# Starting the second half of an expert layer with the two experts whose split weights are still in the ring

## The reference, cut to what matters

```python
x = layernorm(x + linear_attention(x))          # "first" steps b, n
x = layernorm(x + x0_experts(x, token_ids))     # 4 experts, picked by token id
x = layernorm(x + golden_ffn(x))                # f0: 8 experts, all run on all tokens
x = layernorm(x + group_attention(x))           # steps a*.2 to a*.12
x = layernorm(x + cross_attention(x, ctx))      # steps a*.13 to a*.18
x = layernorm(x + moe(x))                       # f1: routed experts and a shared one
```

```python
gate = einsum('btd,edf->betf', x, Wg);  up = einsum('btd,edf->betf', x, Wu)
e_out = einsum('betf,efd->betd', silu(gate) * up, Wd)
out = einsum('bte,betd->btd', weights, e_out)   # weights: the golden router
```

## Time and profile before

| what | value |
|---|---|
| median of three runs | 465.72 us (464.29 to 471.58) |
| the profiled execution: its time | 466.7 us |
| its span, from first to last instruction | 464.9 us |
| outside the span | 1.8 us |
| PE busy | 439.1 us, 94% of the span |
| DVE, ACT, POOL busy | 248.5, 247.2, 261.5 us (53 to 56%) |
| mean granted clock of TensorE | 0.985 |
| transfers | 35.22 MB, 76 GB/s on average |

### The profile page before, as it was taken

The page is one execution under the profiler, slowest core; times in us unless marked ns, Lnnn a source line. Parts: engine busy times, 40 slices in busy tenths (PEclk is TensorE's granted clock), DMA queues, the critical chain, the costliest instruction groups (busy, mean ns, idle before and its releaser), DMA issues.

```text
span 464.9 us, 9286 instructions
## 1 busy us (share of the span) xinstructions
PE 439.1 (94%) x3668; PEld 367.4 (79%) x3668; DVE 248.5 (53%) x625; ACT 247.2 (53%) x424; POOL 261.5 (56%) x217
## 2 busy tenths in 40 slices
...
DMA packets 15672, 35.22 MB, mean 76 GB/s; under 512 B 2028, under 2 KB 5996, under 8 KB 15629
## 3 DMA queue, kind: packets, MB, share of 16 engines
...
q10 hardware_dynamic: 476, 0.63, 0.5%
...
HBM read 33.05 MB, written 1.05 MB: 73 GB/s over the span
## 4 chain that ended last, share of the span: by engine, by line
PE 56%; DVE 4%; ACT 3%; POOL 2%; issue 2%; ACTq 0%; POOLq 0%; DVEq 0%
PE bank L435 11%; PE bank L438 9%; PE bank L436 9%; PE bank L679 5%; PE bank L681 5%; PE bank L680 5%; PE bank L753 2%; PE bank L636 2%; PE bank L741 1%; DVE stats L1301 1%; ACT x_tok L905 1%; POOL rstd L1156 1%; PE bank L725 1%; PE bank L727 1%; PE bank L726 1%
## 5 line engine op out<-in xcount | busy, mean ns | idle before, releaser
L1190 POOL TENSOR_TENSOR h_lo<-hraw,h_hi 128x512 fp32r<-128x512 f32 x76 | 97.8, 1290 | 66.4 <-ACT h_hi L992 66.1
L435 PE MATMUL bank<-xT_hi,pk_hi 128*128 128x512 f32 x256 | 106.1, 414 | 4.0 <-DVE hraw L1476 3.2
L436 PE MATMUL bank<-xT_hi,pk_lo 128*128 128x512 f32 x256 | 101.9, 398 | 1.3 <-issue 1.3
L992 ACT ACTIVATE h_hi<-hraw 128x512 fp32r<-128x512 f32 x76 | 47.8, 629 | 86.3 <-DVE hraw L1476 79.0
L1476 DVE TENSOR_TENSOR hraw<-bank,sil 128x512 f32<-128x512 f32 x76 | 52.3, 689 | 64.0 <-PE bank L438 30.6
L1196 POOL TENSOR_TENSOR pk_lo<-pk_raw,pk_hi 128x512 fp32r<-128x512 f32 (+1 forms) x44 | 74.5, 1694 | 19.1 <-ACT pk_hi L1010 19.0
L438 PE MATMUL bank<-xT_lo,pk_hi 128*128 128x512 f32 x256 | 81.5, 400 | 0.0
L679 PE MATMUL bank<-pk_hi,h_hi 128*128 128x256 f32 x272 | 78.0, 287 | 2.0 <-DVE x_tok L1490 2.0
L681 PE MATMUL bank<-pk_hi,h_lo 128*128 128x256 f32 x272 | 76.8, 283 | 0.0
L680 PE MATMUL bank<-pk_lo,h_hi 128*128 128x256 f32 x272 | 76.8, 282 | 0.0
L435 PEld LDWEIGHTS bank<-xT_hi,pk_hi 128*128 128x128 f32 x256 | 48.7, 190 | 21.9 <-issue 8.8
...
## 6 DMA issues: line engine op xcount, KB each, us to landing
...
```

Source lines behind the costliest of these rows:

```text
L435: pe.matmul(o, w(kc)[0], x(kc)[0], start=kc == 0, stop=False)
L436: pe.matmul(o, w(kc)[1], x(kc)[0], start=False, stop=False)
L992: A(h_hi[:, row, at * 512:(at + 1) * 512], hraw[:, s % 2, :], ACT.Copy).then_inc(sems["hid_hi"], 1)
L1190: pool.tensor_tensor(h_lo[:, row, q], hraw[:, s % 2, :], h_hi[:, row, q].bitcast(F32), ALU.subtract).then_inc(sems["hid_lo"], 1)
```

## The change

The second half of f0 begins with experts 6 and 7, whose split weights are still in the two slots, and goes on with experts 0 to 5. The function `expert` gives the expert of a unit, and DVE takes the router's weights by it. Packs of f0 are numbered 0 to 13 apart from the units (`pack_f0`), and a slot may be overwritten after the last unit that uses its pack (`last_use`). The packs of f1 then have numbers from 14. `chunk`, `pack_f1` and `last_use` are written for f1 as well, but with `RF1 = 0` and both tuples in plain order nothing changes there. Two transfers of 512 KB and two of 256 KB fall away, and with them two copies of each kind on ACT and two subtractions of each kind on POOL. The matmuls are the same in number and size. The five tables of orders are written anew throughout.

```diff
+PK0, RF1 = 2 * E0 - 2, 0
...
+def expert(m):
+
+    return (m if m < E0 else m - 2) % E0
+
+FIRST, SECOND = tuple(range(N1)), tuple(range(N1))
...
+def again(j, n, r):
+
+    return j if j < n else j - r
+
+def last_use(i, n, r):
+
+    return i if i < n - r else i + r
+
+def pack_f0(m):
+    return again(m, E0, 2)
...
-    return ("f0", i) if i < 2 * E0 else ("f1", i - 2 * E0)
+    return ("f0", i) if i < PK0 else ("f1", i - PK0)
...
 DVE_ORDER = """
-p0 b0.0 b0.1 b0.2 b0.3 b0.4 b0.5 p2 b0.6 b0.7 p5 b0.8 b1.0 b1.1 n0.0 b1.2 b1.3 b1.4 b1.5 b1.6 b1.7 n0.2 b1.8 m0 m1
+p0 b0.0 b0.1 b0.2 b0.3 b0.4 b0.5 p2 b0.6 b0.7 b1.0 b0.8 p5 n0.0 b1.1 b1.2 b1.3 b1.4 b1.5 b1.6 b1.7 n0.2 m0 b1.8 m1 m2
...
                 elif u < U_F1:
-                    pe.wait_ge(sems["g_lo"], u - U_F0 + 1)
+                    pe.wait_ge(sems["g_lo"], pack_f0(u - U_F0) + 1)
...
-                    pe.wait_ge(sems["d_lo"], m + 1)
-                    chunks, wh, wl = KC, d_part("f0", m, pk_hi), d_part("f0", m, pk_lo)
+                    i = pack_f0(m)
+                    pe.wait_ge(sems["d_lo"], i + 1)
+                    chunks, wh, wl = KC, d_part("f0", i, pk_hi), d_part("f0", i, pk_lo)
...
                 elif kind == "f0" and i >= 2:
-                    act.wait_ge(sems["up_ready"], up_no(S_F0 + 2 * (i - 2) + 1))
+                    act.wait_ge(sems["up_ready"], up_no(S_F0 + 2 * last_use(i - 2, E0, 2) + 1))
...
-                    act.wait_ge(sems["out_ready"], out_no(U_F0 + i - 2))
+                    act.wait_ge(sems["out_ready"], out_no(U_F0 + last_use(i - 2, E0, 2)))
...
-                    weights, e, h = gold, (u - U_F0) % E0, (u - U_F0) // E0
+                    weights, e, h = gold, expert(u - U_F0), (u - U_F0) // E0
```

More of the change, by code:

```diff
@@ L107 @@
+G17 G18 S4 G19 G20 G21 G22 G23 G24 G25 R1 G26 G27 G28 G29 G30 G31 G32 G33 G34 G35 G36 G37 G38 G39 G40 G41 O0
 """.split()
 PE_ORDER = """
-b0.0 b0.1 b0.2 b0.3 b0.4 b0.5 b0.6 b0.7 b1.0 b0.8 b1.1 b0.9 b1.2 b1.3 b1.4 b1.5 b1.6 b1.7 n0.2 b1.8 g0 g1 b1.9 g2 g3
-d0 g4 n1.2 g5 g6 d1 g7 g8 d2 g9 g10 d3 g11 g12 d4 g13 r0.2 d5 g14 r0.3 g15 g16 u16 d6 g17 d7 u17 g18 u18 g19 u19 d8
-g20 u20 g21 u21 r1.2 d9 r1.3 g22 u22 g23 d10 u23 g24 u24 g25 u25 g26 u26 g27 d11 u27 d12 g28 u28 g29 d13 u29 g30 u30
-g31 u31 d14 d15 g32 u32 g33 u33 a0.2 g34 u34 a0.3 a0.4 d16 a0.5 a0.6 a0.7 g35 a0.8 u35 g36 u36 g37 u37 d17 a0.10 g38
@@ L118 @@
-u74 g75 u75 d48 d49 d50 d51
+b0.0 b0.1 b0.2 b0.3 b0.4 b0.5 b0.6 b0.7 b1.0 b0.8 b1.1 b0.9 b1.2 b1.3 b1.4 b1.5 b1.6 b1.7 n0.2 b1.8 g0 g1 g2 b1.9 g3
+g4 d0 g5 g6 n1.2 d1 g7 g8 d2 g9 g10 d3 g11 g12 d4 g13 g14 r0.2 d5 g15 g16 r0.3 d6 u16 g17 u17 g18 d7 u18 g19 d8 u19
+g20 u20 g21 u21 d9 g22 u22 g23 d10 u23 g24 u24 g25 d11 u25 g26 r1.2 u26 g27 r1.3 d12 u27 g28 u28 g29 u29 d13 g30 u30
+g31 u31 g32 d14 u32 d15 g33 u33 g34 u34 a0.2 g35 u35 a0.3 a0.4 d16 g36 a0.5 a0.6 a0.7 d17 a0.8 u36 g37 u37 g38 u38 g39
@@ new lines @@
+u39 a0.10 d18 a0.25 g40 u40 a0.11 g41 a0.26 d19 u41 g42 u42 g43 u43 a0.14 d20 a0.15 g44 u44 a0.16 g45 u45 a0.17 g46
+a0.18 d21 u46 g47 u47 a0.21 d22 a0.22 d23 g48 u48 g49 u49 g50 u50 a1.2 d24 d25 a0.24 a1.3 a1.4 g51 u51 a1.5 a1.6 a1.7
+d26 a1.8 g52 u52 g53 u53 g54 u54 a1.10 d27 a1.25 d28 g55 a1.11 u55 a1.26 g56 u56 d29 d30 g57 u57 g58 a1.14 d31 d32
+a1.15 u58 d33 a1.16 g59 u59 a1.17 d34 a1.18 g60 u60 g61 u61 a1.21 d35 d36 a1.22 g62 u62 d37 g63 u63 g64 a1.24 u64 g65
+d38 d39 u65 g66 u66 g67 d40 u67 d41 d42 g68 u68 g69 d43 u69 g70 u70 g71 d44 d45 u71 g72 d46 u72 g73 u73 g74 u74 g75
@@ L141 @@
+D40 G41 l71 l72 l73 l74 D41 l75 y0 y1
 """.split()
 DVE_ORDER = """
[L143 to L146 removed]
```

106 lines of the change are left out of this document (54 added, 52 removed).

## The result

The changed kernel takes 470.1 us (median of 4 runs, 468.6 to 470.9); the kernel before, run beside it, 466.1. The ratio is 1.0094, 95% interval 1.0053 to 1.0135. A second series gave 470.45 against 465.79, ratio 1.0084 (1.0046 to 1.0122). The forecast was 464.7, in a range that ended at 468.5. The profiled execution took 470.9 us, its span is 469.1, against 466.7 and 464.9 before.

The account below looks back on a forecast made before the run. PE was taken as the bound, busy 439.1 of 464.9 us. Terms 1.8 + 0.3 - 0.3 - 3.9 + 1.1 = -1.0 took the profiled 466.7 to 465.7, median forecast 464.7 us, range 460.5 to 468.5.

Parts of the forecast that it names:

- New pause before `g2`: Start of f0: `g2` must wait for `m0`, as `b1.9` no longer hides that chain; +1.8 us, bounds 0 and 2.5.
- End of f0's first half: Old pauses of 3.1 us go, new ones before `g31` and `d15` total 3.4; +0.3 us, bounds -3.1 and +1.5.
- `d15`'s: End of f0's first half: a new pause of 2.2 us before `d15`, with `c` taken at 5.55 us.
- Just enough: Before `g21`: PE's 8.5 us of work would cover the 8.3 us of `m18`, router block 0 and `m19`.
- Attention of the first half: Wait at `a0.14` 2.3 us where 3.0 were lost, plus 0.4 for another pause; -0.3 us, bounds -3.0 and +1.7.
- Both sides of that sum: First half's attention: 2.3 us lost by waiting instead of 3.0, against 0.4 for a pause like `g40`'s elsewhere.
- Start of f1: Around `u49`, `g50`: shorter pauses, no low clock, +0.65 for a new `a1.2` wait; -3.9 us, bounds -4.7 and -1.5.
- Smaller ones: Cross attention +0.3, `a1.14` +0.3, pauses between the second half's small matmuls +0.5; +1.1 us together.
- the other two parts: Cross attention's read has less work ahead of it, +0.3 us; `a1.14` has less work over its chain, +0.3 us.
- the second: Rival, chance 0.2: new pauses before `g2` and `d15` also bring low clock, 1.7 us each; 468.1 us.
- The fourth: Rival, chance 0.1: waits behind `u50`, `a1.2` or `a1.3` grow as `u49`'s shrinks; -1.5 for -3.9, 467.1 us.
- term 4: Start of f1: the gain of -3.9 us from shorter pauses before `u49` and `g50` and no low clock.

Follow-up runs that it names:

- e15: Changed kernel with the old start up to `g10`, `h10`, `l8`, `a2`, but ScalarE's `S0` left in its changed place behind `h2`: median 471.6 us.
- e12: Changed kernel repeated with no edit, for a second trace and more runs: semaphore pauses the same to 0.01 us; its median is not given.
- e4: Changed kernel with one GpSimd step moved, `S3` behind `a1.0` instead of ahead of it: gain 0.9 us at equal clock.
- e5: Changed kernel with three GpSimd steps moved away from VectorE's router blocks, `D2` behind `l19`, `D7` behind `l29`, `S3` behind `l48`: median 470.0 us.
- e7: Old order tables without the two dropped packs, with one VectorE swap, `m48` ahead of `a1.0`: median 468.2 us.
- e9: Old tables without two packs; `m48`, `G16` ahead of `a1.0`, `m49` behind; `g50`, `u50` ahead of `a1.2`; `h48`, `h49` ahead of `a1.1`; `S3` behind `l48`: median 465.5 us.

## Why the prediction was wrong, point by point

1. *New pause before `g2`, +1.8*: 1.65. Right; e15 got 1.1 of it back.
2. *End of f0's first half, +0.3*: the old pauses went (3.16) and `g21` 1.14 and `g31` 1.46 came, `d15`'s not: -0.56. The net was near, two parts were wrong for one reason. Block 0 was taken at 6.8 us from the earlier trace rows; here it takes 7.8 (112.09 to 119.91), with 2.1 us of waiting for GpSimd. "Just enough" was not. And `c`, "5.55 us, measured", held 2.6 us of such waits: it takes 2.9 us (169.28 to 172.22) in the changed kernel, so `d15` waits for nothing. The rows of `c`'s longest instruction, before (with GpSimd's beside it) and after:

```profile
157.58 2.77 DVE L1365 TENSOR_SCALAR cap<-cap 128x1024 f32<-128x1024 f32 x1
...
157.40 2.39 POOL L1196 TENSOR_TENSOR pk_lo<-pk_raw,pk_hi 128x1024 fp32r<-128x1024 f32 x1
```

```profile
171.25 0.70 DVE L1402 TENSOR_SCALAR cap<-cap 128x1024 f32<-128x1024 f32 x1
```

3. *Attention of the first half, -0.3*: +0.4 between the profiles, +2.5 in the mean of traces, beyond my bound of +1.7. I had set a missing stretch of low clock in one execution against a pause, as if it belonged to the order. Both sides of that sum were wrong: `a0.14` waits 0.31 us and not 2.3, and the pauses put down to issue did not go but grew, from 1.8 to 2.2 us between the profiles and from 2.0 to 3.0 in the means.
4. *Start of f1, -3.9*: this is the step that failed most. I took the router block for as long as before and put nothing for GpSimd's `S3`, which now runs inside it. `u49` waits 2.13 us instead of 0.8, since one instruction of 0.19 us took 1.65; the clock fell behind it in the profiled execution (not in e12's); `g50`'s 1.04 went as said, and `a1.2` did not wait. That is -1.6 of -3.9. e4 and e5 show the cause: with `S3` behind the block the wait is 0.67. e7 and e9 show that even without the collision the gain needs cover behind it.
5. *Smaller ones, +1.1*: the pauses in the second half's small matmuls are 4.98 us against 2.22: +2.8 where I put 0.5, and +2.1 in the means of eight traces of each order (1.8 and 3.9). That TensorE runs out of instructions was right; that less work between the blocks makes it worse is not shown, and the size was a guess from a single row. Of the other two parts, the cross attention's read waits 0.44 us and `a1.14` not at all.
6. *Not in the list*: `a1.24` and `u64`, 1.05 and 0.85 us, in every trace with the changed tables there and in none with the old. `a1.23` moved behind `m62` and into three of GpSimd's instructions, and lost 2.4 us. No run moved GpSimd away there, so how much of the 1.9 us is the collision and how much the later place stays open. I walked five places and took the rest for unchanged.

With what each measured the six add up to 1.65 - 0.56 + 0.4 - 1.6 + 2.8 + 1.9 = 4.6 us, against 4.2 us in the spans and -1.0 in the forecast.

Of the rivals, the second had the right sign and, at 468.1, nearly the size, for a reason that no run bears out: no low clock follows `g2` or `g31` in any trace. The fourth (term 4 is taken back, 467.1, chance 0.1) is what e7 and e9 show with the old tables; in the changed kernel itself `a1.2` does not wait, and the loss lies ahead of `u49`.
